# A four-layer convolution chain on one core: first image loaded from ScalarE's queue, its transposes moved among the preparing products, three reorderings, and the last stores split over two queues

## What is computed

```
x  = L0(x)   # channel attention (norms of q and k over pixels), residual, 1x1 conv 48+48 -> 96,
             # leaky relu, 3x3 conv 96 -> 96, leaky relu, 1x1 conv 96 -> 48, residual
x  = L1(x)   # relu, depthwise 3x3, 1x1 conv, batch norm
x  = L2(x)   # mean over pixels -> sigmoid routing over 4 experts; the mixed weights do
             # 1x1 conv 48 -> 192, relu, depthwise 3x3 on 192, relu, 1x1 conv 192 -> 48, + x
x  = L3(x)   # relu, depthwise 3x3, 1x1 conv, batch norm
```

## Time and profile before

| | |
|---|---|
| median of 3 runs | 1031.4 us (1030.27 to 1031.84) |
| the profiled execution's own time | 1031.31 us |
| its span, first to last instruction | 1029.5 us |
| TensorE's mean granted clock | 0.979 of full speed |
| busy: TensorE, VectorE, ScalarE, GpSimd | 93%, 84%, 47%, 8% |

### The profile page before, as it was taken

One profiled execution on the slowest core, in us unless ns is written; L12 is line 12 of the kernel. 1 busy time (PEld: TensorE's weight loads), 2 busy tenths in 40 slices (PEclk: granted clock), 3 DMA queues, 4 the chain that ended last, 5 costly groups with the idle time before them and its releaser, 6 DMA issues.

```text
span 1029.5 us, 15286 instructions
## 1 busy us (share of the span) xinstructions
PE 962.1 (93%) x4854; PEld 612.6 (60%) x4854; DVE 862.1 (84%) x1229; ACT 483.3 (47%) x827; POOL 78.3 (8%) x112
## 2 busy tenths in 40 slices
PE   4599969999999999999999999999999999988986
PEld 3456645666665675666665675666665675655534
DVE  5763679998799969998799979998799979989960
ACT  3221445364724655264724655265724656234531
POOL 0120012000300012000300012000300002000000
PEclk9699989999999999999999999999999999989999
DMA  5152815187516655187516655187526655155214
GB/s 75 38 136 55 150 49 131 30 134 158 131 47 107 132 125 131 27 131 161 128 50 105 134 126 132 26 131 162 122 55 104 133 125 136 27 115 120 44 39 98
DMA packets 129520, 104.49 MB, mean 101 GB/s; under 512 B 97903, under 2 KB 98772, under 8 KB 129492
## 3 DMA queue, kind: packets, MB, share of 16 engines
q1 hardware_dynamic: 129492, 104.14, 48.8%
HBM read 10.82 MB, written 6.29 MB: 17 GB/s over the span
## 4 chain that ended last, share of the span: by engine, by line
PE 72%; DVE 11%; ACT 5%; SPq 4%; issue 4%; DMA 3%; ACTq 0%; DVEq 0%
PE bank L1318 27%; PE bank L1354 9%; PE bank L1298 5%; PE bank L1324 4%; DVE dwa L715 3%; PE bank L1422 3%; PE bank L1357 3%; PE bank L1356 3%; PE bank L1338 3%; PE bank L1369 3%; PE bank L1370 3%; PE bank L1288 2%; DMA y_parts<-a_parts 2%; SPq L1025 2%; PE bank L1400 2%
## 5 line engine op out<-in xcount | busy, mean ns | idle before, releaser
L715 DVE SCALAR_TENSOR_TENSOR dwa<-h1a,dyn,dwa 128x1024 f32<-128x1024 f32 x224 | 279.7, 1274 | 3.8 <-ACT dwa L1605 3.0
L1318 PE MATMUL bank<-y_parts,w_l 128*96 128x512 f32 x576 | 149.7, 404 | 0.5 <-issue 0.4
L1318 PE MATMUL bank<-y_parts,w_h 128*96 128x512 f32 x576 | 147.6, 400 | 0.0
L715 DVE SCALAR_TENSOR_TENSOR dwb<-h1b,dyn,dwb 128x1024 f32<-128x1024 f32 x112 | 142.6, 1273 | 0.0
L1168 POOL TENSOR_TENSOR y_low<-y,y_parts 96x512 fp32r<-96x512 f32 x56 | 73.7, 1317 | 780.0 <-DVE y L769 780.0
L1318 PEld LDWEIGHTS bank<-y_parts,w_l 128*96 128x96 f32 x576 | 90.7, 162 | 61.6 <-issue 22.5
L1354 PE MATMUL bank<-a_parts,wt_h 128*112 128x512 f32 x384 | 117.8, 415 | 7.7 <-DMA y_parts<-a_parts 7.4
L1318 PEld LDWEIGHTS bank<-y_parts,w_h 128*96 128x96 f32 x576 | 93.0, 161 | 44.3
L1354 PEld LDWEIGHTS bank<-a_parts,wt_h 128*112 128x112 f32 x384 | 63.7, 177 | 43.8 <-issue 22.3
L1298 PE MATMUL bank<-xq,w_cur 97*96 97x512 f32 x128 | 67.8, 611 | 3.4 <-DVE y L769 3.4
L1640 ACT ACTIVATE y<-bank,b2s 96x512 f32<-96x512 f32 x32 | 21.9, 684 | 102.5 <-PE bank L1324 102.5
(11 more groups left out here) (265 smaller groups left out, 1615.5 us busy)
## 6 DMA issues: line engine op xcount, KB each, us to landing
y_parts<-y_parts SPq DMA_DIRECT2D x32, 396.0 KB, 3.5
y_parts<-a_parts SPq DMA_DIRECT2D x64, 198.0 KB, 3.0
y_parts<-a_parts SPq DMA_DIRECT2D x64, 197.6 KB, 3.5
tok<-in_x_dram SPq DMA_DIRECT2D x48, 192.0 KB, 4.9
y_parts<-y_low SPq DMA_DIRECT2D x64, 132.0 KB, 3.4
a_parts<-a_parts SPq DMA_DIRECT2D x128, 66.0 KB, 2.4
x_even<-y_parts SPq DMA_DIRECT2D x32, 198.0 KB, 3.5
x_odd<-y_parts SPq DMA_DIRECT2D x32, 198.0 KB, 4.0
```

The lines of the kernel that those rows point to most:

```text
L715: nc.vector.scalar_tensor_tensor(out=dst, in0=tap_input(n, t), scalar=weight, in1=dst, op0=ALU.mult, op1=ALU.add).then_inc(tap_step, 1)
L1318: nc.tensor.matmul(bank[0:C2, :], wgt[:, t, :], y1_parts[:, part, rows, cols], start=part + t == 0, stop=False)
```

## The change

Seven things are changed:

1. `load_x(act, 0)` is the first thing in ScalarE's program; SP no longer issues image 0.
2. TensorE transposes chunks 0 and 1 of image 0 after the products L1191 and L1192, and chunks 2 and 3 after L1195; ScalarE copies them out without waiting for the mark `attention`.
3. The clearing L552 to L555 becomes `prepare_places` and stands after conv1 of image 0.
4. In iteration 0 VectorE runs `mix_weights` ahead of `norms_of_q`, `norms_end` behind `norm_of_k`, and `mix_project` with `project_weights` behind the second `h1b_rows`. ScalarE has `route` ahead of `fourth_powers`.
5. In the last iteration `l1_low_part(f, 3)` stands after the first of the three taps of `BY_PROJECT + 1`.
6. ScalarE's `project_affine(f, IMAGES, 2)` stands ahead of `last_finish(5)`.
7. The last image's stores: SP stores chunks 0 and 1 once both are there, then of chunks 2 and 3 the half of j = 0; ScalarE issues the half of j = 1.

```
@@ vector: prepare_conv2
+            def prepare_places():
                 for tile in (wt_h[L1], wt_h[L3], wt_l[L1], wt_l[L3]):
                     step(nc.vector.memset(tile[:, :, :].bitcast(F32), 0.0))
                 step(nc.vector.memset(beside_f, 0.0))
                 ...
@@ vector: iteration, back is None
                     sums_out(attn)
+                    mix_weights(f)
                     norms_of_q(attn)
-                    mix_weights(f)
-                    mix_project(f)
-                    project_weights()
-                    norms_end(attn)
...
                 halo_out(f)
                 norm_of_k(attn)
+                if back is None:
+                    norms_end(attn)
                 h1b_rows(f, 0)
                 conv1_weights(attn)
                 h1b_rows(f, 1)
+                if back is None:
+                    mix_project(f)
+                    project_weights()
                 conv1_out(attn, f)
@@ vector: last_iteration
-                depthwise_at(back, BY_PROJECT + 1)
+                depthwise_at(back, BY_PROJECT + 1, steps=slice(0, 1))
                 l1_low_part(f, PCHUNKS - 1)
+                depthwise_at(back, BY_PROJECT + 1, steps=slice(1, None))
@@ vector: main
             conv1_out(0, None)
+            prepare_places()
             prepare_norms()
@@ sync
-            load_x(sp, 0)
...
-            store(sp, LAST, range(3))
-            store(sp, LAST, range(3, 4))
+            store(sp, LAST, range(2))
+            store(sp, LAST, range(2, 4), steps=(0,))
@@ tensor
             nc.tensor.matmul(banks[3][0:C, 0:C + 1], wqkv[:, 2 * C:3 * C], ...)
+            transpose_x(0, (0, 1))
             pe.wait_ge(prep_dve, marks["wv_t"])
             ...
             nc.tensor.matmul(banks[4][0:C, 0:C + 1], wln[:, :], wv_t[:, :], ...)
+            transpose_x(0, (2, 3))
             pe.wait_ge(prep_dve, marks["p1"])
...
-            transpose_x(0, range(4))
             attention_scores(0, range(4))
@@ scalar
+            load_x(act, 0)
             act.wait_ge(prep_dve, marks["variance"])
             nc.scalar.activation(inv96[0:C, L0:L0 + 1], ...Sqrt)
-            act.wait_ge(prep_dve, marks["attention"])
...
-                if back is None:
-                    fourth_powers(attn)
                 route(f)
-                if back is not None:
-                    fourth_powers(attn)
+                fourth_powers(attn)
...
+                project_affine(f, IMAGES, 2)
                 last_finish(5)
-                project_affine(f, IMAGES, 2)
                 project_affine(f, IMAGES, 3)
                 ...
+                act.wait_ge(ot_ready, 4 * IMAGES)
+                store_chunks(act, f, range(2, 4), (1,))
             x_out(0, range(4))
+            act.wait_ge(prep_dve, marks["attention"])
             scores_out(0, range(8))
```

More of the change, by code:

```diff
@@ L1184, in _, with transpose_x @@
         def _(pe):
+            def transpose_x(image, chunks):
+                for n in chunks:
+                    if n == 0:
+                        pe.wait_ge(xt_loaded, 16 * XT_LOADS * (image + 1))
+                        after(pe, one_placed, image)
+                    bank = ring_a.take(pe, image, A_XT + n)
+                    for m in range(4):
+                        i = 4 * n + m
+                        both_rows = columns(tok[:, :, :, :], (2 * i + 1) * TOK + X_AT - ODD_AT, [[1, P2]])
+                        last = nc.tensor.transpose(bank[0:P2, m * 128:(m + 1) * 128], both_rows, ident[:, :])
+                    last.then_inc(xt_done, 1)
             pe.wait_ge(norm_loaded, 16 * NORM_LOADS)
@@ L1216, in prepare_biases @@
                                      start=True, stop=True).then_inc(prep_pe, 1)
-            def transpose_x(image, chunks):
-                for n in chunks:
-                    if n == 0:
-                        pe.wait_ge(xt_loaded, 16 * XT_LOADS * (image + 1))
-                        after(pe, one_placed, image)
-                    bank = ring_a.take(pe, image, A_XT + n)
-                    for m in range(4):
-                        i = 4 * n + m
-                        both_rows = columns(tok[:, :, :, :], (2 * i + 1) * TOK + X_AT - ODD_AT, [[1, P2]])
-                        last = nc.tensor.transpose(bank[0:P2, m * 128:(m + 1) * 128], both_rows, ident[:, :])
-                    last.then_inc(xt_done, 1)
             def attention_scores(image, rounds):
```

30 lines of the change are left out of this document (15 added, 15 removed).

## The result

Six runs of the changed kernel have a median of 1022.7 us (1020.0 to 1026.1), those of the kernel before 1031.3. The ratio is 0.9921 (0.9906 to 0.9936), a gain of 8.1 us with an interval of 6.6 to 9.7, where 13.0 were forecast. The direction was right; the size was not, and 1022.7 lies just outside the range of 1014.5 to 1022.5.

What follows compares the result with a forecast made beforehand. TensorE was taken to hold 72% of the chain of waits, with gains only in the pipeline's two ends: 4.3 + 2.9 + 3.3 + 0.3 + 2.2 = 13.0 us, giving 1018.3 us, range 1014.5 to 1022.5.

Steps and rivals of the forecast that it cites:

- the gain goes through: Last iteration, change 5: the time won at L1's chunk 2 reaches the end of the kernel; 3.3 us, at most 3.7.
- The rival with this place: Last iteration passes no gain on: copies land no earlier, or the clock falls anyway and later waits fill; 1021.6, chance 0.1.
- wait for each other there by less than a us: Last iteration behind L1's chunk 2: VectorE and TensorE form one chain to the end, each waiting under a us.
- the slow clock as a cost of the wait: L1's chunk 2: with the wait cut from 3.10 to 0.6 us, the clock stays high, chunk about 2.9 us shorter.
- the squares are done 5.33 us later: Preparation: from scores starting at about 18.7, squares finish at 24.0 and norms begin at about 24.0, gaining 4.3 us.
- 0.9 us for the fold's later start: Preparation: issuing x from ScalarE delays the fold's first product by 0.9 us, bounds 0 and 2.0.
- my rival for "slower": Preparation: batch norm's eight small loads queue behind x's and start the fold late, VectorE's clearing covering 2.5 us; chance 0.02.
- The clearing behind conv1: Clearing needs 4.7 us where VectorE waited 3.48; `prepare_norms` is 1.2 us late, hidden, with no new TensorE wait.
- the table's place and the root: ScalarE's start: table load follows the six transfers of x, and the root is ready at 8.0 to 9.2 us.
- iteration 0 by its steps: Iteration 0, change 4: earlier mixing and halo let q's transposes start sooner; 2.9 us gained, bounds 2.0 and 3.5.
- the stores: Kernel's end, change 7: half the bytes stored early, two issues per queue behind the last copy; 2.2 us, bounds 1.5 and 2.7.
- no effect on the loop: Iterations 1 to 6: nearly all TensorE, nothing of the change runs there, so 0 us.

Runs made afterwards that it cites:

- v_last: Changed kernel with two more last-iteration moves: low part of L3's chunk 1 earlier, ScalarE's relu of unit 4 ahead of L3's chunk 0 and the sigmoid; 1018.4 us.
- v_best: `v_last` with changes 1 and 2 undone: x back on SP, transposes behind the products, clearing still behind conv1; 1017.3 us.
- a_no5: Changed kernel with change 5 undone: low part 3 behind all three taps again; 1022.8 us.
- p_swap: Kernel before with change 6 alone: affine step of projection 2 ahead of the last relu; 1030.5 us.
- p_iter0: Kernel before with change 4 alone: the new order in iteration 0; 1027.5 us.
- p_store: Kernel before with change 7 alone: half of the last stores early, the rest on SP and ScalarE; 1028.8 us.
- p_half: Kernel before with the last stores as in change 7, but all issued on SP; 1029.1 us.
- p_queue: Kernel before with changes 1 and 3: x from ScalarE's queue and later clearing, transposes still behind the products; 1029.3 us.
- p_front: Kernel before with changes 1 to 3 alone: x from ScalarE's queue, transposes among the products, later clearing; 1027.9 us.
- p_low3: Kernel before with change 5 alone: low part 3 two taps earlier in the last iteration; 1030.3 us.
- p_23: Kernel before with changes 2 and 3: transposes among the products and later clearing, x still on SP; 1028.5 us.
- p_clear: Kernel before with change 3 alone: clearing behind conv1, x on SP, transposes behind the products; 1028.1 us.
- after: First profile of the changed kernel, all seven changes against the kernel before; profiled execution 1021.38 us, median of six runs 1022.7 us.
- v_fin: Changed kernel with one further move alone: ScalarE's relu of unit 4 ahead of L3's chunk 0 and the sigmoid; 1022.0 us.
- again: The changed kernel, unaltered, timed and profiled once more; 1023.4 us.

## Why the prediction was wrong

**Wrong: "the gain goes through" (last iteration, 3.3 forecast, nothing measured).** The rival with this place had the right result and half the reason: the copies did land earlier, and later waits filled up. The step that failed is the chain behind L1's chunk 2. It was said that VectorE and TensorE wait for each other there by less than a us. But L3's chunk 0 waits for VectorE's list: its low part 1 started 60.3 us after conv2's first product in both profiles (918.20 and 913.05), untouched by the change, and in the changed kernel its copies let TensorE go on at +68.0. Behind that stands ScalarE's order: the sigmoid with its table load of 1.28 us ahead of the relu that the projection needs, 3.21 us of idle TensorE in every profile with the old order. The two moves of `v_last` shortened just these waits, and in its profile and `v_best`'s the stage from c7 to h7 is 4.4 us shorter than in the mean without, where change 5 alone had gained nothing.

**Wrong in the same term: the slow clock as a cost of the wait.** In the earlier trace rows L1's chunk 2 ran at half clock behind the wait, and I took the one for the price of the other. With change 5 undone, `a_no5` has nearly the same wait, 2.75 us, and full speed behind it. What decides the stage is what the projections do behind their 3.21 us of idle time. In the kernel before and `p_swap` they start 77.7 to 77.8 us after c7 and are done in 3.6. In four profiles with chunk 2 slow for part of its time (`p_iter0`, `p_store`, `p_half`, `p_queue`) they start at 76.1 to 76.4 and take 5.3. With chunk 2 at full speed they take 5.0 to 5.2 in `p_front`, `p_low3` and `p_23`, and 6.3 to 6.6 in `p_clear`, `a_no5` and the changed kernel's two, where they start at 75.1 to 76.7 and run at half speed for most of the time. So of the up to 2.7 us by which TensorE is early there (in `p_low3` it is 0.6 late), 1.4 to 2.9 are given back, and the profiled execution of before, with 81.35 us from c7 to h7, was an average one (81.6), although its clock was slow just where I looked. The forecast removed one slow stretch and did not ask whether the next idle time would bring another. Why the clock falls behind some of these waits and not behind others stays open.

**Wrong: "the squares are done 5.33 us later" (preparation, 4.3 forecast, 2.6 measured).** This step failed: in the changed kernel's two profiles VectorE could begin the norms only 7.15 and 8.28 us after the scores' start (24.60 - 17.45 and 27.11 - 18.83), since TensorE ran the scores at half clock, in part or throughout. They took 5.9 to 7.1 us in all seven profiles with the transposes among the products, and 4.1 to 4.8 in eight of the nine without. So all that TensorE's new order gained, with scores that in `after` even started 1.2 us ahead of the forecast, was given back. The forecast carried the 5.33 us over from a profile in which the clock was high for the scores, and did not ask when it would rise with other work ahead of them. In the eight it rose at 18.5 to 20.6 and stayed up until the scores were done. In `after`, `v_last` and `p_front` it rose at 15.6 to 16.1, behind the spread transposes, and fell again at 19.0 to 19.5, when less than half of the scores were done. In the other five it did not rise before 33.5. The ninth without spread transposes, `p_low3`, is one of these five (7.1 us, hidden under the clearing), so the slow scores are a matter of likelihood and not of a rule; what decides it stays open.

The other term of the sum, 0.9 us for the fold's later start, had the right size by luck: it moved by 0.6 to 1.4 us, 0.9 in the mean of the six profiles with changes 1 to 3. I had priced ScalarE's root. In five of the six what came last was the batch norm's small loads, which land 2.8 to 3.5 us later beside x; only in `v_fin` (and in `p_queue`, with change 1 but not 2) did VectorE then wait for the root, 0.27 and 0.40 us. The loads were my rival for "slower": the mechanism is real, and VectorE's cover took all but this. The Trainium skill's place for the table load (ScalarE: Activation LUTs, "Step-by-step: what each stage is for") fits the trace (6.65, behind the transfers). By the profiles, changes 1 and 2 were worth nothing or less beside the clearing, which alone gives 3.8.

**Right.** The clearing behind conv1 cost nothing; the table's place and the root; iteration 0 by its steps, 3.3 against 2.9 and inside its bounds; the stores, 2.0 against 2.2; and no effect on the loop. The 1.8 us that the first profile seemed to lose in the loop (1.6 of them in iteration 1) was scatter.

**Mis-sized: change 6.** 0.5 to 1.0 us by the stages at equal clock and 0.9 (-0.2 to 2.2) by the times, against 0.3. I took too little, since the stall of SP's issue (2.50 us) seemed a matter of one execution. This gain and the 0.4 us too many in iteration 0 hid a part of what the last iteration and the preparation fell short.

## What to carry to other kernels

A wait that is taken away at one place of a chain is worth only the distance to the next thing that sets the time there: look for each later wait of the same engine, and ask what releases it and whether that release moves at all. Here change 5 alone took one wait away and gained nothing; only with the next two shortened as well was there a gain. And before a stretch at half clock is priced as a gain, look at the same stretch in several executions, and at the next idle time behind it, which may bring another.

## What the runs showed of the hardware that was not expected

**The first stretch of a trace has no clock record.** A row's clock is worked out from the trace's records of it, and where there is none it prints 1.00. In all 16 traces the first record is a rise to 1.00, somewhere between 15.6 and 38.4 us. In `again` it stands at 34.6, so the 1.00 in the first row below is no measurement: the 64 scores take 7.15 us, 421 ns each. In `p_queue` the clock rose at 19.5, the 1.00 is a record, and the same products take 4.14 us:

```profile
18.80:26.00 7.20, 7.15 (x64) 6.91 (x64) 4.03 (x10) 2.99 (x12) 0.00 (x0) 1.00 0.13 31
```

```profile
19.70:24.10 4.40, 4.14 (x65) 3.77 (x64) 0.90 (x4) 3.49 (x15) 0.00 (x0) 1.00 0.03 4
```

The durations say that TensorE was at 1.2 GHz until the first record. In `after` eight scores take 0.45 to 0.52 us in the stretch recorded at 1.00 and 0.85 to 0.96 in that at 0.50; in `again` they take 0.85 to 0.96 throughout. The transposes of the kernel before, sixteen in 3.81 us at 15.43, are twice as fast 97 us later:

```profile
112.28 1.03 PE L1228 MATMUL bank<-ident,tok 128*112 128x128 f32 x8
```

The Trainium skill (TensorE: Matmul & The Clock Gate, "Seeing it yourself") warns that this chip's records of the clock can be unreliable; no run here shows that, as the scores' durations fit the record wherever there is one. Ahead of the first record, the mean duration of a product of known shape is the witness to go by.

**What came ahead of fast and slow scores.** Directly ahead of the fast scores TensorE had made 16 transposes without a pause; ahead of the slow ones it had waited 0.90 us, but for `p_low3`, whose scores were slow without that wait.

**Transfers on a second queue delay small ones.** Six large transfers issued on ScalarE's queue at 0.75 us delayed eight small ones, issued on SP from 0.76 us on, by 2.6 to 3.5 us: TensorE's first product started at 4.35 us in `p_clear` and at 6.95 to 7.88 with change 1. SP issued the last of the eight only 0.3 us later (3.19 to 3.21 instead of 2.93), so nearly all of the delay came after the issue: queues that are separate in issue were not separate in transfer.
